# Order of the first loads, and the table of the last four scatters, in a four-layer kernel with a mixture of experts

## The reference

```python
x = L0_attn_x                                    # (16, 256, 256) float32
x = _layernorm(x + _L0_attn_ref(x, ...))         # a chunked state space layer, 64 heads
x = _layernorm(x + _L0_ffn_ref(x, ...))          # SwiGLU with integer weights, 704 wide
x = _layernorm(x + _L1_attn_ref(x, ...))         # cumulative attention and SwiGLU, 1024 wide
x = _layernorm(x + _L1_ffn_ref(x, ...))          # mixture of experts
```

```python
logits = xf @ gate_inp.T
topv, topi = jax.lax.top_k(logits, K)            # K = 4 of E = 16
w = jax.nn.softmax(topv.astype(jnp.float32), axis=-1)
u = jnp.einsum('nc,ehc->neh', xf, W_up)          # C = 256, H = 448
g = jnp.einsum('nc,ehc->neh', xf, W_gate)
h = jax.nn.silu(g) * u
y = jnp.einsum('neh,ech,ne->nc', h, W_down, dense_w)
```

## Time and profile before

| | us |
|---|---|
| three runs, median (lowest to highest) | 2051.32 (2050.51 to 2056.98) |
| the profiled execution, its own time | 2047.72 |
| its span, first to last instruction | 2045.9 |
| PE / DVE / POOL / ACT busy | 1778.9 / 1319.3 / 856.9 / 730.6 |
| first matmul starts | 14.04 |
| last scatter starts | 1994.68 |
| first instruction of POOL in the combining block | 2004.99 |
| mean granted clock of TensorE | 0.946 |

### The profile page before, as it was taken

The page is one execution under the profiler, slowest core; times in us unless marked ns, Lnnn a source line. Parts: engine busy times, 40 slices in busy tenths (PEclk is TensorE's granted clock), DMA queues, the critical chain, the costliest instruction groups (busy, mean ns, idle before and its releaser), DMA issues. The chain is left out here.

```text
span 2045.9 us, 34902 instructions
## 1 busy us (share of the span) xinstructions
PE 1778.9 (87%) x8724; PEld 1228.7 (60%) x8725; DVE 1319.3 (64%) x2876; ACT 730.6 (36%) x1384; POOL 856.9 (42%) x856
## 2 busy tenths in 40 slices
PE   3589999999999899999999998874899999999980
PEld 2257667666576676766766766653456666666650
DVE  3778878778788787788887878532344444444445
ACT  3244344344443443444434434221222233232323
POOL 1133243333432433334324333222466676666654
PEclk8799999999999999999999999977899999999995
DMA  8223132231331322313313223083999999999997
GB/s 284 62 93 101 36 108 66 79 108 37 98 108 27 108 63 81 108 37 98 108 27 112 70 70 103 21 260 99 232 169 170 173 179 175 175 177 176 177 152 252
DMA packets 385800, 244.37 MB, mean 119 GB/s; under 512 B 269072, under 2 KB 364624, under 8 KB 385360
## 3 DMA queue, kind: packets, MB, share of 16 engines
q1 hardware_dynamic: 319952, 171.79, 32.6%
q0 software_dynamic: 40704, 67.40, 17.7%
q10 hardware_dynamic: 25088, 4.50, 1.2%
HBM read 119.23 MB, written 67.73 MB: 91 GB/s over the span
## 5 line engine op out<-in xcount | busy, mean ns | idle before, releaser
L1663 PE MATMUL pu<-w_all,xh 128*128 x1728 | 363.6, 357 | 44.9 <-DMA xh<-xin 32.0
L1663 PEld LDWEIGHTS pu<-w_all,xh 128*128 128x128 bf16 x1728 | 168.6, 98 | 196.9 <-issue 75.9
L1796 POOL DMA_INDIRECT sums_dram<-yo,meta_in x144 | 229.0, 1591 | 136.6 <-issue 71.2
L1749 DVE TENSOR_TENSOR hid<-pu,gate 128x448 f32<-128x448 f32 x144 | 90.0, 625 | 251.8 <-PE pu L1663 130.2
L826 PE MATMUL pb<-x1T,w_sw 128*128 128x256 f32 x1024 | 230.9, 384 | 0.9 <-ACT x1T L944 0.7
L826 PEld LDWEIGHTS pb<-x1T,w_sw 128*128 128x128 f32 x1024 | 193.7, 191 | 46.5 <-issue 15.5
L1678 PE MATMUL py<-w_all,hh 112*128 x1728 | 212.6, 273 | 1.4 <-DMA hh<-hs 1.4
L1678 PEld LDWEIGHTS py<-w_all,hh 112*128 112x128 bf16 x1728 | 168.8, 98 | 45.1 <-issue 2.2
L1783 POOL DMA_INDIRECT xin<-x_dram,meta_in x144 | 142.3, 988 | 63.8 <-issue 47.0
L642 PE MATMUL pa<-w_in,xT 128*128 128x512 f32 (+1 forms) x384 | 156.0, 552 | 14.7 <-DMA xT<-in_xT 14.0
L1313 DVE SCALAR_TENSOR_TENSOR y<-v,small,y 128x512 f32<-128x512 f32 x224 | 157.8, 746 | 1.2
(11 more groups left out here) (244 smaller groups left out, 3178.1 us busy)
## 6 DMA issues: line engine op xcount, KB each, us to landing
w_stage<-in_w_ug SPq DMA_DIRECT2D x64, 224.0 KB
split_ug<-w_parts SPq DMA_DIRECT2D x64, 224.0 KB
w_all<-split_ug SPq DMA_DIRECT2D x16, 896.0 KB, 9.1
xg_dram<-xg SPq DMA_DIRECT2D x16, 512.0 KB, 3.5
rows<-sums_dram SPq DMA_DIRECT2D x32, 256.0 KB, 5.3
w_stage<-in_w_dn SPq DMA_DIRECT2D x32, 224.0 KB
split_dn<-w_parts SPq DMA_DIRECT2D x32, 224.0 KB
w_all<-split_dn SPq DMA_DIRECT2D x16, 448.0 KB, 10.5
```

What stands on the lines that cost most here:

```text
L1663: last = mm(pu[:, 2 * b + w, 0:EH], xh[:, m % XS, DC * xp + c, :], w_ug[:, bass.ds(e, 1), wp, c, w * EH:(w + 1) * EH], start=n == 0, stop= ...
L1749: vec.tensor_tensor(hid[:, :], pu[:, 2 * (m % 2), 0:EH], gate[:, :], ALU.mult).then_inc(hid_ready.sem, 1)
L1796: nc.gpsimd.indirect_dma_start(out=sums_dram[m % 2], out_offset=bass.IndirectOffsetOnAxis(ap=meta[:, m, 0:1], axis=0), in_=yo[:, m % XS, : ...
```

## The change

Four things change.

1. The first loads are reordered. `load_x(0)` is issued ahead of everything; then come the five loads of a new list `loads_first` (`w_in`, `small`, `dt_bias`, `neg_a`, `bc_bias`), counted by `first_loaded`; then the rest of `loads`. PE's first piece, ACT and DVE wait for `first_loaded`; PE's and DVE's piece A2 of sequence 0 waits for `setup_loaded`, and DVE's copy of `count_mats` goes there. POOL's `select` waits for `setup_loaded` as before.
2. `loads_b`, the padding and its 17 stores leave `load_rows` and become the piece AR (`load_rest`) of SP's row, behind WL.1. The first two pieces of expert weights stay in `load_rows`.
3. With `LAST = 4`, tiles 140 to 143 all add into table 1. Each of these waits for the tile just before it; all others wait for the tile two before, as they did.
4. SP issues one load at the end of the experts' block, after its last transpose and a wait for tile 138: all 4096 rows of table 0 (4096 KB, 32 rows of 1 KB in each partition) go to `rows_first`, which begins at `w_start`, over the weights of experts 0 to 2. The combining block loads one table's rows for each sequence instead of two, and adds those of `rows_first`. DVE waits for `rows_first_in` once, ahead of the first sequence.

```diff
@@ ORDER
-    "SP": ("CE C7 A0 N0 A2 WL.0 WL.1 C9 WL.2 WL.3 WL.4 WL.5 CF"),
+    "SP": ("CE C7 A0 N0 A2 WL.0 WL.1 AR C9 WL.2 WL.3 WL.4 WL.5 CF"),
@@ build
+        rows_first = nc.alloc_sbuf_tensor_at("rows_first", [P, nseq, NT, D], F32, offset=w_start)
@@ layers_block, sync
+            def load_rest(s):
+
+                if not isinstance(s, int) or s > 0:
+                    return
+                for to, src in loads_b:
+                    sp.dma_start(to, src).then_inc(weights_loaded.sem, 16)
+                sp.dma_start(padding[:, :, :], ins["empty"]).then_inc(padding_in.sem, 16)
+                sp.wait_ge(nothing_set.sem, nothing_set.at(0))
...
+            load_x(0)
+            for to, src in loads_first:
+                sp.dma_start(to, src).then_inc(first_loaded.sem, 16)
+            for to, src in loads:
+                sp.dma_start(to, src).then_inc(setup_loaded.sem, 16)
@@ layers_block, tensor g1
-                    pe.wait_ge(setup_loaded.sem, setup_loaded.at(0))
+                    pe.wait_ge(first_loaded.sem, first_loaded.at(0))
@@ experts_block
+        def into(r, m):
+
+            i = UN * r + m
+            if isinstance(i, int) and i >= ntile - LAST:
+                return 1, (ntile - LAST) // 2 + i - (ntile - LAST)
+            return m % 2, pair(r, m)
...
+        def same_table(r, m):
+
+            i = UN * r + m
+            back = 1 if isinstance(i, int) and i >= ntile - LAST else 2
+            return added(r + (m - back) // UN, (m - back) % UN)
@@ experts_block, sync, after its steps
+            sp.wait_ge(*added((ntile - LAST - 2) // UN, (ntile - LAST - 2) % UN))
+            sp.dma_start(rows_first[:, :, :, :].rearrange("p s t d -> p (s t) d"),
+                         sums_dram[0][0:ntok, :].rearrange("(s p) d -> p s d", p=P)).then_inc(rows_first_in.sem, 16)
@@ experts_block, gpsimd scatter
-                    pool.wait_ge(y_stored[m % 2].sem, y_stored[m % 2].at(pair(r, m) - 1))
+                    pool.wait_ge(*same_table(r, m))
@@ combine_block, sync
-                for n, sums in enumerate(sums_dram):
-                    sp.dma_start(rows[:, m, n, :, :], sums[bass.ds(i * T, T), :].rearrange("(t p) d -> p t d", p=P)
-                                 ).then_inc(loaded[m].sem, 16)
+                sp.dma_start(rows[:, m, :, :], sums_dram[1][bass.ds(i * T, T), :].rearrange("(t p) d -> p t d", p=P)
+                             ).then_inc(loaded[m].sem, 16)
@@ combine_block, vector
+                if isinstance(i, int) and i == 0:
+                    dve.wait_ge(rows_first_in.sem, rows_first_in.at(0))
```

More of the change, by code:

```diff
@@ L48 @@
 WS = 4
+LAST = 4
 WU, WD = 2 * DC * 2 * EH, 2 * EJ * D
@@ L256, in build @@
         experts_block(nc, ntok, cap, ntile, ident, waited, small, base, table, meta_dram, x3_dram, sums_dram, split_ug, split_dn,
-                      w_all, weights_in)
-        combine_block(nc, nseq, waited, sums_dram, out)
+                      w_all, weights_in, rows_first, rows_first_in)
+        combine_block(nc, nseq, waited, sums_dram, out, rows_first, rows_first_in)
 SM_P, SM_E, SM_TRI, SM_HALF = 0, 1, 1 + NE, 1 + NE + NE * NE
@@ L410, in mat @@
             return const[:, k, :]
[L412 to L415, removed]
+        loads_first = [(w_in[:, :, :], ins["w_in"].rearrange("(c p) n -> p c n", p=P)), (small[:, :], ins["small"]),
+                       (dt_bias[:, :], ins["dt_bias"]), (neg_a[:, :], ins["a_log"]), (bc_bias[:, :, :], ins["bc_bias"])]
+        loads = [(const[:, :, :], ins["matrices"]), (ident, ins["matrices"][:, IDENT, :]),
+                 (chosen_rows[:, :], ins["chosen_rows"]), (right[:, :], ins["right"]), (halves[:, :, :, :], ins["halves"]),
                  (w_out[:, :, :], ins["w_out"].rearrange("(c p) n -> p c n", p=P))]
@@ L551, in load_rows @@
                 if isinstance(s, int) and s == 0:
-                    for to, src in loads_b:
-                        sp.dma_start(to, src).then_inc(weights_loaded.sem, 16)
                     load_piece(0, 0)
                     load_piece(0, 1)
[L557 to L564, removed]
+            def load_rest(s):
[5 more added lines that the diff above has]
+                sp.wait_ge(nothing_set.sem, nothing_set.at(0))
+                for sums in sums_dram:
+                    sp.dma_start(sums[nseq * T:nseq * T + P, :], nothing[:, 0:D]).then_inc(sums_cleared.sem, 16)
+                sp.wait_ge(padding_in.sem, padding_in.at(0))
+                for e in range(NE + 1):
+                    sp.dma_start(meta_dram[e * cap:(e + 1) * cap, :].rearrange("(p i) w -> p i w", p=P),
+                                 padding[:, :, :]).then_inc(padding_stored.sem, 16)
             def store_x3(s):
@@ L669, in a2 @@
             def a2(s):
+                if isinstance(s, int) and s == 0:
+                    pe.wait_ge(setup_loaded.sem, setup_loaded.at(0))
                 pe.wait_ge(steps_ready.sem, steps_ready.at(s))
@@ L1210, in a2 @@
             def a2(s):
+                if isinstance(s, int) and s == 0:
+                    dve.wait_ge(setup_loaded.sem, setup_loaded.at(0))
+                    vec.tensor_copy(count_mats[:, :, :], const[:, STRICT:ONES + 1, :])
                 ca.start(s)
@@ L1526, in load_weights, with experts_block @@
                  ).then_inc(weights_in[e % WS].sem, 16)
-def experts_block(nc, ntok, cap, ntile, ident, waited, small, base, table, meta_dram, x3_dram, sums_dram, split_ug, split_dn, w_all, weights_in):
+def experts_block(nc, ntok, cap, ntile, ident, waited, small, base, table, meta_dram, x3_dram, sums_dram, split_ug, split_dn, w_all, weights_in, rows_first, rows_first_in):
     with ExitStack() as ctx:
@@ L1574, in pair, with added @@
             return UN // 2 * r + m // 2
+        def into(r, m):
[3 more added lines that the diff above has]
+            return m % 2, pair(r, m)
+        def added(r, m):
+            n, k = into(r, m)
+            return y_stored[n].sem, y_stored[n].at(k)
+        def same_table(r, m):
+            i = UN * r + m
+            back = 1 if isinstance(i, int) and i >= ntile - LAST else 2
+            return added(r + (m - back) // UN, (m - back) % UN)
         def steps(eng, run, first, last):
@@ L1796, in scatter @@
                 nc.gpsimd.indirect_dma_start(
-                    out=sums_dram[m % 2], out_offset=bass.IndirectOffsetOnAxis(ap=meta[:, m, 0:1], axis=0),
+                    out=sums_dram[into(r, m)[0]], out_offset=bass.IndirectOffsetOnAxis(ap=meta[:, m, 0:1], axis=0),
                     in_=yo[:, m % XS, :], in_offset=None, compute_op=ALU.add
-                ).then_inc(y_stored[m % 2].sem, 16)
+                ).then_inc(y_stored[into(r, m)[0]].sem, 16)
             def step(r, m):
@@ L1806, in _, with combine_block @@
             steps(pool, step, -4, ntile + 4)
-            for n in range(2):
-                pool.wait_ge(y_stored[n].sem, y_stored[n].at(ntile // 2 - 1))
-def combine_block(nc, nseq, waited, sums_dram, out):
+            for i in (ntile - LAST - 2, ntile - 1):
+                pool.wait_ge(*added(i // UN, i % UN))
+def combine_block(nc, nseq, waited, sums_dram, out, rows_first, rows_first_in):
     CS = 4 if nseq % 4 == 0 else 1
@@ L1819, in sig @@
             return Signal(ctx.enter_context(nc.semaphore(name)), per)
-        rows = sb("rows", [P, CS, 2, NT, D])
+        sb("rows_room", [P, nseq, NT, D])
+        rows = sb("rows", [P, CS, NT, D])
         res = sb("res", [P, CS, NT, D])
@@ L1826, in combine_block @@
         fin = sb("fin", [P, CS, NT, D])
-        loaded = [sig(f"loaded{n}", 32) for n in range(CS)]
+        loaded = [sig(f"loaded{n}", 16) for n in range(CS)]
         summed = sig("summed", 1)
@@ L1887, in sums @@
                     dve.wait_ge(normed.sem, normed.at(i - CS))
-                vec.tensor_tensor(res[:, m, :, :], rows[:, m, 0, :, :], rows[:, m, 1, :, :], ALU.add
-                                  ).then_inc(summed.sem, 1)
+                first = rows_first[:, i, :, :] if isinstance(i, int) else rows_first[:, bass.ds(i, 1), :, :]
+                vec.tensor_tensor(res[:, m, :, :], rows[:, m, :, :], first, ALU.add).then_inc(summed.sem, 1)
                 dve.wait_ge(summed.sem, summed.at(i))
```

14 lines of the change are left out of this document (7 added, 7 removed).

## The result

The changed kernel took 2064.13 us (median of 19 runs, 2045.37 to 2072.5), the kernel before 2050.51 us in 19 runs (2041.24 to 2056.98). The ratio is 1.0055, with a 95% interval of 1.0038 to 1.0072: 11 us slower (8 to 15). The prediction had 2054.3 us, in a range of 2046.5 to 2062.5. The median of the changed kernel lies 1.6 us above the end of that range; the ratio applied to the 19 runs before gives 2061.8 us, just inside it. So the range held by a hair at best. The likeliest case of the prediction, a time that can't be told from no change, is not what came. What came is its two slower rivals at once: the dragged scatters, stronger than priced, and the longer stay of SP in AR.

A forecast was written before the change was run, and what follows sets the result against it. PE was taken as the bound nearly everywhere, with the change touching only the two ends. Start -4.9 and end +7.9 (10.5 - 2.6) gave +3.0 on the 2051.3 us median: 2054.3 us, range 2046.5 to 2062.5.

The forecast's parts named there:

- The likeliest case of the prediction: Whole kernel: a time within about 0.3% (6.2 us) of no change, chance 0.62; the forecast itself was 2054.3 us.
- the dragged scatters: Slower rival, end: load of `rows_first` drags three chained scatters to 6.75 us each; +7.3 us, 2058.6 us, chance 0.20.
- the longer stay of SP in AR: Slower rival, start: SP held longer in AR, WL.4 at 77.3, lead only 1.1 us; +6.8, 2058.1 us, chance 0.08.
- (a): Start, first loads: 705 KB less ahead of PE's first matmul, which starts at about 8.6 us, 5.4 us earlier.
- (b): Start, SP's queue: `xg` stored at 30.6 instead of 41.06, so `u` at 42.4 instead of 54.41, 12.0 us earlier.
- (c): Start, SP in AR until 68.6: DVE's WL.4 waits until 73.5, so 4.9 of the 12.0 us lead is left.
- slow bound: Start: all 7.45 MB beside AR move at 324 GB/s, so WL.4 comes at 77.3 and the lead is 1.1 us.
- (d): End, tiles 140 to 143 chained: 4.67 us between dependent scatters in a quiet queue, last scatter 8.6 us late.
- (e): End, scatters beside the `rows_first` load: 5.3 us per link, bounds 3.35 and 6.75; last scatter 10.5 us late.
- p: End: time from the start of one chained scatter to the start of the next, which waits for it; taken as 5.3 us.
- (f): Combining block: one load for the first sequence, then DVE's pace of 1.85 us per sequence; 2.6 us less together.
- worst joint case: Both ends at their slow bounds: +12.2 at the end, only 1.1 us lead at the start, +11.1; top of the range.

## Where the prediction held and where it failed

**(a), the first loads: right.** 8.6 foretold, 8.29 and 8.47 measured.

**(b), `u` 12 us earlier: half right.** `xg` was stored at 31.23 (30.6 foretold), but `u` came only 6.4 us earlier. Two things were mis-sized. The first is in the sum: it let `u` gain 12.0 us where `xg` gains 10.5. From the issue of `xg` to `u` it took 11.8 us, where the earlier trace rows have 54.41 - 41.06 = 13.4; its step from that issue to the first gather, 3.9 us, was 5.4 before and 4.5 after. The second is `loads_b` beside the gathers: from `xg` to `u` it is 16.8 us in the changed kernel and 13.9 with `loads_b` out of the way, where `u` came 9.5 us earlier. The prediction had named this as the reason, should `u` be late, but gave it no price.

**(c), the lead is lost to AR: the mechanism was right, its size too small.** SP was free at 72.03, not 68.6, and ACT had the piece 4.5 us after its issue, not 3.5. The transfer term is what was mis-sized: from `w_gate` to the end of the wait for `padding` it took 24.8 us, where 21.6 had been worked out at 391 GB/s. WL.4 came at 77.96, where 73.5 was foretold and 77.3 was the slow bound. The lead was 0.4 us, just outside the bounds of 1.1 to 9.5. The slow bound used the 324 GB/s of the combining block, and that would have come nearer, at 23.0 + 2.5 = 25.5 us. So the 4.9 us that the sum counted on were not there, and the rival of the longer AR came true.

**(d), one link of the chain 4.67 us: right** (4.54 to 4.63 in a quiet queue); the first link, beside the last transposes, took 5.4.

**(e), p = 5.3 beside the load: wrong,** and this is the step that decided the sign. Beside the load a link takes 7.6 to 8.6 us. The upper bound of 6.75 was too low as well: it came from plain stores of `out`, and the adding scatter is dragged by 3 to 4 us where I allowed 2. What makes it so much more than the store of `out`, no run tells. The load landed after 15.9 us, so the fourth link was quiet again, at 4.70 us; a fourth dragged link would have cost 3 to 4 us more. The three links together took 20.9 us, where 15.9 was foretold.

**(f), the combining block 2.6 us shorter: right.** 1.8 us shorter than in the profile of before: sequence 0 came 0.8 us sooner, as foretold, but from there to sequence 15 it took 2057.55 - 2028.91 = 28.6 us, not 27.75. Over all executions with two loads for a sequence (40.8 to 42.5 us from the block's start to the end of the span) against those with one (39.1) it is 1.7 to 3.4.

**The sum.** Foretold -4.9 + 10.5 - 2.6 = +3.0; by the traces -0.4 + 16.2 - 1.8 = +14.0; by the time of many runs +11 (8 to 15). That the time comes so near to the range is luck: it was as wide as its worst joint case, +11.1, and just that case came, with (c) and (e) both beyond their bounds. The step that failed is the price of a link beside the load, p in (e). The rival of the dragged scatters was to be told from the forecast at p = 6.4, and p was between 7.6 and 8.6. It had a chance of 0.20 and should have had more: in the earlier trace rows the one row that showed a transfer beside others, the stores of `out`, was the nearest row, and I took a value below it because a scatter has half the bytes. The transfer with half the bytes was dragged more, not less.

The fit that the Trainium skill gives in DMA: Bandwidth & Descriptors, in its section on the anatomy of one DMA on the GpSimd path (2.0 us plus bytes over 436 GB/s), makes an estimated 2.3 us for a scatter of 128 KB. The quiet link of 4.6 us less the 1.55 us of POOL's own part leaves 3.0, in which the landing and POOL's start on the next scatter are not told apart; so the fit comes out lower than this trace. The Trainium skill's DMA: Bandwidth & Descriptors has, in its section on latency, 0.2 us for an access to DRAM on average and 2 us at high load. Here the load added 3.0 to 4.0 us to a link, which may hold more than one access; so the direction agrees and the size is larger.

## What to carry to other kernels

A load that is pulled forward under a chain of dependent small DMAs is not free: here each link beside it took 7.6 to 8.6 us instead of 4.6. So price the chain with a loaded row, and above it rather than below. And what stands ahead in an issuer's list is counted in the issuer's time, its waits and its many small stores too: with the new first loads, two pieces of SP's list moved further back made the kernel 11 us faster, where the rearranged end made it 13 us slower. Before shortening the wait for a first load, see whether the next wait is for the queue, as it was here.

## What the hardware showed that was not expected

- An indirect, adding scatter of 128 rows of 1 KB takes 4.5 to 4.7 us from its start to the start of one that waits for it; beside a 4 MB load from DRAM 7.6 to 8.6 us, whether that load reads the other table or an unrelated tensor. The cost of the load and that of the chain added up (6.7 and 9.1 apart, 15.9 to 16.2 together, each from one profiled execution).
- The load of 4 MB in rows of 1 KB was issued in 0.58 us and landed in 15.4 to 16.9 us, some 250 to 270 GB/s, while the issue of a 16 KB table behind 6 MB of loads held SP for 8.0 to 8.6 us in every execution. So it is not the size of a DMA alone that holds its issuer. What is still queued ahead of it is the likely reason, and the load of `w_so` points the same way: its issue took 1.47 us before and 2.80 after, where gathers and pieces of expert weights were in flight with it. But no run put the table anywhere but behind these loads, so that is not shown.
